# Six row maxima of the attention layer moved into the last quad of the layer before it, and the late groups' projections and splits spread over later rows

## The reference, cut to what matters

```python
# layer 1: norm, input projection, depthwise 3x3 conv, a state-space mix, norm, output projection, x += out
# layer 2: x += Wo(attention(norm(x))), 8 heads of 8 channels, 256 positions an image:
q, k, v = heads(xn @ Wq + bq), heads(xn @ Wk + bk), heads(xn @ Wv + bv)
out = softmax(q @ k.T / sqrt(8)) @ v
# layer 3: x += deformable 3x3 convolution(norm(x)), offsets and masks from two 3x3 convolutions
```

## Time and profile before

| what | us |
|---|---|
| median of 3 runs | 499.68 |
| the profiled execution's own time | 501.63 |
| its span in the trace | 499.8 |
| TensorE busy | 426.8 (85%) |
| VectorE busy | 348.5 (70%) |
| ScalarE busy | 277.9 (56%) |
| GpSimd busy | 126.4 (25%) |
| layers 2 and 3's block begins at | 199.2 |
| first exponential (row 0) | 229.60 |
| first normalization (row 13) | 240.11 |

### The profile page before, as it was taken

One profiled execution on the slowest core, in us unless ns is written; L12 is line 12 of the kernel. 1 busy time (PEld: TensorE's weight loads), 2 busy tenths in 40 slices (PEclk: granted clock), 3 DMA queues, 4 the chain that ended last, 5 costly groups with the idle time before them and its releaser, 6 DMA issues.

```text
span 499.8 us, 9219 instructions
## 1 busy us (share of the span) xinstructions
PE 426.8 (85%) x3374; PEld 227.8 (46%) x3374; DVE 348.5 (70%) x688; ACT 277.9 (56%) x512; POOL 126.4 (25%) x163
## 2 busy tenths in 40 slices
PE   0525876899999998658998999998999999799997
PEld 0214756745555575223434343444534455355442
DVE  4638886522345677687998978979677687568785
ACT  1179984114035255324877877966287496476441
POOL 4330002200000002036653313124048066056000
PEclk9855998799999999695999999999999999889999
DMA  5400000550000043424430204405902832822500
GB/s 149 124 1 1 0 0 1 110 100 0 1 0 1 13 145 96 127 63 127 111 87 3 55 13 107 102 3 145 231 7 66 207 66 72 188 47 67 139 12 10
DMA packets 22090, 34.97 MB, mean 70 GB/s; under 512 B 5184, under 2 KB 18912, under 8 KB 20512
## 3 DMA queue, kind: packets, MB, share of 16 engines
q1 hardware_dynamic: 19696, 27.68, 22.2%
q0 software_dynamic: 1200, 5.44, 4.2%
q10 hardware_dynamic: 1152, 1.29, 1.2%
HBM read 16.78 MB, written 5.24 MB: 44 GB/s over the span
## 4 chain that ended last, share of the span: by engine, by line
PE 40%; DVE 9%; DMA 4%; POOL 2%; issue 2%; SPq 2%; ACT 1%; DVEq 0%; ACTq 0%; POOLq 0%
PE L_banks L1845 10%; PE L_banks L1745 7%; PE L_banks L1712 6%; PE L_banks L1819 5%; DVE L_mx L1323 3%; PE L_banks L1791 3%; DMA L_hats<-L_parts 2%; PE L_banks L1783 2%; DMA L_hat<-L_offsets 2%; SPq L1189 1%; PE L_banks L537 1%; PE L_banks L1725 1%; PE L_banks L1756 1%; PE L_banks L1767 1%; PE L_banks L1733 1%
## 5 line engine op out<-in xcount | busy, mean ns | idle before, releaser
L1323 DVE TENSOR_REDUCE L_mx<-L_banks 128x2 f32<-128x512 f32 x128 | 84.8, 687 | 20.5 <-PE L_banks L1712 19.5
L1460 DVE TENSOR_TENSOR L_s<-L_banks,L_cols 128x1024 f32<-128x1024 f32 x72 | 87.6, 1219 | 9.6 <-PE L_banks L1819 8.1
L1492 ACT ACTIVATE L_e<-L_banks 128x512 f32<-128x512 f32 x128 | 72.9, 597 | 30.2 <-PE L_banks L1725 24.9
L1845 PE MATMUL L_banks<-L_s,L_t_sb 128*64 128x256 f32 x576 | 79.4, 397 | 1.5 <-DVE L_s L1460 1.4
L1574 ACT ACTIVATE L_cols<-L_banks 128x512 f32<-128x512 f32 x72 | 42.8, 595 | 44.2 <-PE L_banks L1832 43.6
L1712 PE MATMUL L_banks<-stacks_k_st,stacks_q_st 64*128 64x256 bf16 x256 | 48.8, 293 | 6.3 <-DVE L_mx L1323 5.0
L1845 PEld LDWEIGHTS L_banks<-L_s,L_t_sb 128*64 128x64 f32 x576 | 35.4, 138 | 35.7 <-DVE L_s L1460 20.9
L1725 PE MATMUL L_banks<-stacks_q_st,stacks_k_st 64*128 64x256 bf16 x256 | 47.7, 284 | 1.4 <-ACT L_e L1492 1.4
L1819 PE MATMUL L_banks<-L_hats,L_sel 48*128 48x512 bf16 x144 | 43.8, 385 | 0.0
L1745 PE MATMUL L_banks<-L_e,L_v_x 128*32 128x256 f32 x512 | 41.9, 399 | 0.0
L1791 PE MATMUL L_banks<-all_w_all,L_xn 64*128 64x192 f32 x192 | 33.6, 346 | 3.3 <-ACT L_cols L1574 3.2
(11 more groups left out here) (286 smaller groups left out, 760.5 us busy)
## 6 DMA issues: line engine op xcount, KB each, us to landing
L_hat<-L_offsets SPq DMA_DIRECT2D x6, 576.0 KB, 6.3
L_hats<-L_parts SPq DMA_DIRECT2D x16, 216.0 KB, 9.4
L_stack<-L_xpad SPq DMA_DIRECT2D x12, 162.0 KB, 3.1
L_stack<-L_xpad SPq DMA_DIRECT2D x12, 153.0 KB, 3.7
L_mask<-L_masks SPq DMA_DIRECT2D x3, 576.0 KB, 9.4
L_hats<-L_parts SPq DMA_DIRECT2D x24, 72.0 KB, 3.0
L_hats<-L_parts SPq DMA_DIRECT2D x12, 144.0 KB, 3.1
L_q_parts<-L_parts SPq DMA_DIRECT2D x8, 192.0 KB, 2.9
```

What stands on the lines that cost most here:

```text
L1323: dve.tensor_reduce(mx[:, n % 2, :, head], ring[:, place["largest", step] % 3].rearrange("p (q s) -> p q s", q=2), AX.X, ALU.max).then_inc ...
L1460: dve.tensor_tensor(s[:, q], row_ps[:, q], cols[:, t % 3:t % 3 + 1].broadcast_to([P, 2, 2 * N]), ALU.mult).then_inc(prod_ready, 1)
L1492: act.activation(e[:, k], ring[:, 3 + v % 3], ACT.Exp, scale=HD2 ** -0.5).then_inc(e_ready, 1)
L1845: mm = pe.matmul(acc[C * half:C * half + C, b, 0:N], t_sb[:, b, h, (KK * half + t) * C:(KK * half + t + 1) * C], s[:, q, h, half * N:(half ...
```

## The change

Three things are moved.

1. **Six maxima steps go to layer 1.** The block of layers 2 and 3 now starts at row -13 (`ROWS[EARLY:]`, EARLY = 6). Steps 0 to 5 stand in quad 3, into PSUM banks of layer 1: steps 0 and 1 right behind the output projection, step 2 behind the sums of squares, steps 3 to 5 at the end. TensorE waits for group 0's stacks in the middle of quad 3. SP sends and loads q of group 0 first, then k.
2. **Layer 1's quad 3 is reordered.** The k split and the values of group 0 move from the end of quad 2 into quad 3; the statistics of x of quads 2 and 3 and the k split and values of group 1 move behind quad 3's addition; one ScalarE table load is dropped.
3. **Groups 2 and 3.** Their lines are made by ScalarE, the projections are spread over rows -5, -4, -2 and -1, the splits stand at rows 3, 6, 9 and 12, the values at rows 8 and 11 (GpSimd's last parts follow in its images 1 and 2, the loads in images 3 to 6). `full` and `rest` have memory of their own instead of lying in `e`, so ScalarE's wait for all parts ahead of row 0 is gone. TensorE runs two `keep_clock` matmuls in each of rows -13 to -6.

```diff
+    def largest(self, pe, step, out):
+        n, k = divmod(step, 8)
+        h, p = k % 2, k // 2
+        for q in range(2):
+            mm = pe.matmul(out[:, q * N:(q + 1) * N], self.rows_of(self.q_st, n, h, p)[:, q * P:(q + 1) * P], self.rows_of(self.k_st, n, h, p),
+                           start=True, stop=True)
+        mm.then_inc(self.max_ps, 1)
+    def late_line(self, act, turn, x, p, out):
+        act.wait_ge(self.norm, self.done(turn, self.SHIFT))
+        act.activation(out, x[:, p, :], ACT.Identity, scale=self.scale[:, p:p + 1], bias=self.shift[:, p:p + 1]).then_inc(self.xn_ready, 1)
+EARLY = 6
 # layer 1, SP
-                stacks.store_parts(sp, 0, parts[:, 0])
-                stacks.load_stacks(sp, 0, 0)
-                stacks.load_stacks(sp, 0, 1)
+                for s in range(2):
+                    stacks.store_parts(sp, 0, parts[:, 0], (s,))
+                    stacks.load_stacks(sp, 0, s)
 # layer 1, VectorE: quad 3 (g = 1)
                     if g >= 0:
+                        if g:
+                            split(0, 1)
+                            stacks.take_values(dve, 0, b_v, bc_ps[:])
                         stacks.shifts(dve, g, pairs)
...
                     dve.tensor_copy(o[:], k_ps[:]).then_inc(o_copied, 1)
+                    for step in range(2 if last else 0):
+                        stacks.take_largest(dve, step, early[step % 3])
                     dve.wait_ge(var_ready, q + 1)
...
                 over_deviation(NQ - 1)
                 add(NQ - 1)
+                for q in range(NQ - 2, NQ):
+                    statistics(q)
+                split(1, 1)
+                stacks.take_values(dve, 1, b_v, bc_ps[:])
+                for step in range(3, EARLY):
+                    stacks.take_largest(dve, step, early[step % 3])
 # layer 1, ScalarE
-                    act.preload_act_table_set("natural_log_exp_and_others")
+                    if not last:
+                        act.preload_act_table_set("natural_log_exp_and_others")
 # layer 1, TensorE, quad 3
+                    else:
+                        pe.wait_ge(acts_ready, 2 * q + 2)
+                        pe.wait_ge(stacks.stacked[0], LOADS * 16)
+                        for step in range(2):
+                            stacks.largest(pe, step, early[step])
 # layers 2 and 3: the table of rows (LAG = 19, FIRST = EARLY - LAG = -13)
-    PROJECT_AT = {-LAG + 7: 2, -LAG + 8: 3}
-    SPLIT_AT = {-LAG + 9: (2, 0), -LAG + 10: (2, 1), -LAG + 11: (3, 0), -LAG + 12: (3, 1)}
+    PROJECT_AT = {FIRST + 8: (2, 0), FIRST + 9: (2, 1), FIRST + 11: (3, 0), FIRST + 12: (3, 1)}
+    SPLIT_AT = {3: (2, 0), 6: (2, 1), 9: (3, 0), 12: (3, 1)}
 # ScalarE
-                    if v == 0:
-                        act.wait_ge(stacks.parts_ready, 2 * NQ)
 # TensorE
+                    elif v < min(PROJECT_AT):
+                        keep_clock(pe, avg2, ring[:, 5], 2)
```

More of the change, by code:

```diff
@@ L523, in shifts, with line @@
     def shifts(self, dve, turn, pairs):
[L525 removed]
         dve.wait_ge(self.norm, self.done(turn, self.SCALE))
[L527 to L530 removed]
+        dve.tensor_tensor(self.shift[:, pairs], self.minus_mean[:, pairs], self.scale[:, pairs], ALU.mult).then_inc(self.norm, 1)
+    def late_line(self, act, turn, x, p, out):
+        act.wait_ge(self.norm, self.done(turn, self.SHIFT))
+        act.activation(out, x[:, p, :], ACT.Identity, scale=self.scale[:, p:p + 1], bias=self.shift[:, p:p + 1]).then_inc(self.xn_ready, 1)
+    def line(self, dve, turn, x, p, out):
+        dve.wait_ge(self.norm, self.done(turn, self.SHIFT))
         dve.tensor_scalar(out, x[:, p, :], self.scale[:, p:p + 1], self.shift[:, p:p + 1], ALU.mult, ALU.add).then_inc(self.xn_ready, 1)
@@ L570, in take_values, with store_parts @@
                           b_v[:, :].unsqueeze(1).broadcast_to([P, 4, P]), ALU.add).then_inc(self.v_all_ready, 1)
-    def store_parts(self, eng, g, parts):
-        for s in range(2):
+    def store_parts(self, eng, g, parts, which=(0, 1)):
+        for s in which:
             eng.wait_ge(self.parts_ready, 2 * g + s + 1)
@@ L872, in quad @@
                     if g >= 0:
-                        stacks.mean(pe, avg2, g, pairs, bc_ps[:, 0:2])
+                        stacks.mean(pe, avg2, g, pairs, small(g))
+                    if g > 0:
+                        pe.wait_ge(stacks.hi_ready, 2 * g)
+                        stacks.values(pe, g - 1, w_v, lines[:, 2 * g - 2:2 * g], bc_ps[:])
                     pe.wait_ge(bt_copied, q + 1)
@@ L1264, in _ @@
                         variance(n // 4 - 1)
-                    if n < 2:
-                        for s_ in range(2):
-                            stacks.last_part(pool, n + 2, s_, rest[:, n, s_], parts[:, n + 2, s_])
                     if n > 1:
@@ L1704, in largest @@
                 def largest(step):
-                    n, k = divmod(step, 8)
-                    h, p = k % 2, k // 2
                     at = place["largest", step]
-                    if step % 32 == 0:
+                    if step and step % 32 == 0:
                         pe.wait_ge(stacked[step // 32], LOADS * 16)
                     bank_free(at)
-                    for q in range(2):
-                        mm = pe.matmul(ring[:, at % 3, q * N:(q + 1) * N], rows_of(q_st, n, h, p)[:, q * P:(q + 1) * P], rows_of(k_st, n, h, p),
-                                       start=True, stop=True)
-                    mm.then_inc(max_ps, 1)
+                    stacks.largest(pe, step, ring[:, at % 3])
                 def scores(v):
```

150 lines of the change are left out of this document (81 added, 69 removed).

## The result

| | before | after |
|---|---|---|
| median of 4 runs, us | 499.61 (498.82 to 500.26) | 508.42 (508.15 to 508.69) |
| profiled execution: own time; span | 501.63; 499.8 | 508.69; 506.6 |
| block of layers 2 and 3 begins | 199.23 | 206.61 |
| first exponential (row 0) | 229.60 | 228.89 |
| first normalization (the mark) | 240.11 | 246.62 |

The ratio is 1.018, 95% interval [1.016, 1.020]: 1.8% slower, where 496.5 us was forecast. Comparisons with an interval leave disturbed runs out (single runs of the kernel before at 789 to 1417 us among them); where a kernel's runs spread over two groups, I give all of them.

A forecast was written before the change was run, and what follows sets the result against it. Ahead of the mark TensorE, then VectorE, then row 0's wait for GpSimd were taken as limits. Block 8.4 us later at 207.6, plus 29.3, puts the mark at 236.9, 3.2 earlier: 499.68 - 3.2 = 496.5 us, range 495.2 to 498.1.

The forecast's parts named there:

- Layer 1, the transfers: Quad 3: TensorE stands 3.9 us (189.8 to 193.7) behind the output projection, until group 0's loads land.
- Low clock behind the wait, 2.0 us dearer: Layer 1 after the stand: k projection, sums of squares and two maxima at half clock take 4.6 us; variance at 198.3.
- the rival that it is kept: TensorE keeps its clock through layer 1's wait: block begins at 205.6, time 494.5 us; chance 0.20.
- Tail of 9.3 us: Layer 1 from the variance on VectorE to the block of layers 2 and 3: 9.3 us, block at 207.6.
- Rows -13 to -1, 13.9 us: From the block's start, seven maxima, norm, lines, then TensorE's projections: row 0's maximum ready at 13.9 us.
- The slower rival: Low clock lasts into rows -13 to -1: row 0 8.1 us later, time 504.6 us; chance 0.14.
- Rows 0 to 13, 15.4 us: VectorE alone without gaps: 14 maxima 9.2, four splits 4.7, two values 1.4, gap 0.1; mark at 29.3.
- the second rival: Rows 0 to 13 don't pack: half of 5 us, 2.5, is added, time 499.0 us; chance 0.24.
- The splits without GpSimd: Rows 0 to 13: subtractions about 0.7 instead of 1.07 us; 1.5 us saved, 1.5 worse if GpSimd still meets them.
- Block's start to mark, 29.3 us: Layers 2 and 3, block's start to first normalization: 29.3 us where it took 40.9, 11.6 saved.

The follow-up runs named there:

- e2: Changed kernel with 30 instead of 20 keep_clock matmuls at the end of layer 1; median 499.02 us, ratio to before 0.999.
- e5: Changed kernel unaltered, run once more; 500.1, 501.6, 509.2 and 510.1 us.
- e6: Changed kernel with group 0's wait and first three maxima behind quad 3's sums of squares, 27 keep_clock matmuls ending layer 1; 494.50 us.
- e13: Changed kernel with 29 keep_clock matmuls at the end of layer 1 and repeated maximum and scores matmuls in rows 4 to 7; 498.41 us.
- e12: e6 with one keep_clock matmul instead of two in each of rows -13 to -6; 496.60 us.
- e16: e10 again, on one chip with e15; 493.28 us, ratio to before 0.987.
- e9: e6 with three of the four values matmuls of groups 2 and 3 left out in rows 7 and 10; 495.47 us.
- e15: e6 again, unaltered; 495.03 us, ratio to before 0.991.
- e8: e6 with the two matmuls of each maximum done twice in rows 0 to 5; 495.41 us.
- e10: e6 with the maximum's matmuls done twice and the scores' three times in rows 4 to 7; 494.66 us.
- e4: Changed kernel with none of the six maxima in layer 1, so 19 rows ahead of row 0 again; 505.22 us.
- e11: Changed kernel with 10 instead of 20 keep_clock matmuls at the end of layer 1; 507.15 us.
- e3: Changed kernel with the wait for group 0's stacks and the first three maxima behind quad 3's sums of squares; 503.52 us.
- e1: Changed kernel without the two keep_clock matmuls in each of rows -13 to -6; 500.69 us, ratio to before 1.002.
- e7: e3 without the keep_clock pairs in rows -13 to -6; 495.64 us, ratio to before 0.990.
- e14: Kernel before with two keep_clock matmuls in each of rows -19 to -13 and 23 instead of 20 ending layer 1; 504.03 us.

## Why the prediction was wrong

- **Layer 1, the transfers**: right. TensorE was to go on at 193.7 after 3.9 us; it did at 192.90 after 3.77. The output projection, said to stay at 189.16 or to come 0.4 sooner, came at 188.05; from its start to the block's it is 18.56 us, where the sum has 18.44.
- **Low clock behind the wait, 2.0 us dearer**: right. Projection 2.07 and sums of squares 1.98 against 1.13 and 1.08 in the earlier trace rows, sum +1.8 us; every profile with the early wait shows some microseconds of half clock here, so the rival that it is kept falls (it had 0.20). Variance on VectorE at 197.5 (said 198.3).
- **Tail of 9.3 us**: right, 9.1 (197.47 to 206.61). But this is the step in which the miss begins. The sum priced the tail as VectorE's and did not look at TensorE beside it: its 20 keep_clock matmuls last 4.7 us and end 2 us ahead of the block. Before, the same matmuls ended 0.90 us ahead of TensorE's next one, as the trace shows; 2.3 us more of tail could not leave that as it was.
- **Rows -13 to -1, 13.9 us**: this step failed. At full clock the first exponential came 14.83 us behind the block's start (e2, e5, e6, e13); in the first profile 22.28. The slower rival, given 0.14, had the mechanism and the size (+8.1; measured 7.45); its time, 504.6, lacks the second stretch. My argument against it, "here it has dense work from 193.7 on, with keep_clock at the end of layer 1 and in each row", took keep_clock's presence for its effect. In the sum itself the pairs stood at nothing. At full clock 0.9 us remain, and TensorE is the likely cause: maximum and pair take 0.96 us a row (207.71 to 208.67), where I let VectorE pace seven of them at 0.66, and with one matmul fewer a row (e12) the way is 1.1 us shorter.
- **Rows 0 to 13, 15.4 us**: the size was off by 2.3 in the first profile and 3.9 in e5, as the second rival said (+2.5). The mechanism of packing was right: with the clock kept it took 15.76. A cause that I had not named, a fall of the clock in these rows, made most of the gaps: e2 and e13 differ here by the filled rows 4 to 7, and need 19.40 and 15.75 us.
- **The splits without GpSimd**: right. A subtraction takes 0.68 us in the rows, and 1.07 in the mean before. One by one the four took 0.68, 1.66, 1.27 and 0.68 us before, and the two long ones (at 216.59 and 219.23) ran beside GpSimd's last parts (216.56 to 217.70, 218.79 to 219.95); in the profile after none of the four does. The Trainium skill, page "GPSIMD Engine Reference", section "Specifications", says that the two contend for their interface to SBUF when VectorE's instruction has two inputs there; the traces agree.
- **Block's start to mark, 29.3 us**: 30.6 at full clock (e13, e16), 40.0 in the first profile. So of the 9.7 us by which the mark was late, 9.4 are the low clock in two stretches, 1.3 the terms just named, and -1.0 the earlier block. The times don't close as well: the mark of e13's profile is 2.2 us ahead of the forecast one, since the output projection started at 186.03 there, and its median of 498.4 is 1.9 us above the forecast of 496.5. So the gain of 3.2 us that was forecast doesn't show in e13's twelve runs either.

What stays open: why the identical kernel lost the clock in six of eight runs and not in two. The runs show only that its stand at the change of blocks lies between a length that kept the clock in every profile of the new order and one that lost it. The changed kernel itself was not run in the series of e2 and e11; the kernel before, with medians of 499.6 to 500.6 in all four series, is what ties them together. Of the 2.4 us by which e9 fell back behind e15 after the mark, 1.3 are the slow stretch up to the second normalization; the rest has no cause here.

## What to carry to other kernels

A filler that keeps TensorE's clock must last as long as what it covers: when a change makes another engine's tail longer, lengthen the filler by as much, and look for the next stretch in which the engine is thin. A filler inside a chain is paid in full once the clock has fallen (0.71 us became 1.22 in each row), so it belongs where TensorE waits, not in front of what others wait for. A wait for a transfer belongs behind all work that doesn't need it (about 4.5 us here). Where a kernel's runs fall in two groups, as here, look at the clock of each run, and time it in more than one series before believing a gain or a loss of 2%: the first four runs here all fell in one group.

## What the runs showed of the hardware

- TensorE's clock fell to half 2.3 us after the engine had gone back to dense work behind a stand of 2.05 us (206.76 to 209), and came back only at 226, though the engine was busy in all of the 17 us between. The same instructions had kept it at 1.00 in e5. The profile's busy column alone doesn't tell when a clock comes back.
- With a stand of 0.45 to 0.48 us at the change of blocks the clock was kept ahead of row 0 in all nine profiles of the new order that have it (e2, e6, e8, e9, e10, e12, e13, e15, e16); with 3.16 and 4.16 us it fell (e4, e11); from 1.81 to 2.08 us it went both ways (kept in e5 at 1.81; fallen in e3 at 1.98 and in the first profile at 2.05, and, without the pairs in the rows, in e1 at 1.84 and in e7 at 2.08). In the old order 0.45 us was not enough: in e14 two waits of 0.62 and 0.48 us followed, and the clock fell at about 203.5.
- A VectorE subtraction of two SBUF tiles (128x512, float32) took 0.68 us with GpSimd still, and 1.27 and 1.66 us beside a GpSimd instruction (216.59 and 219.23 in the trace before).
